# Cross-attention and experts of a decoder layer in one program, with a transition written out by hand

## What is computed

```python
x = _layernorm(x + _L0_attn_ref(x, wq, wk, wv, wo))
x = _layernorm(x + _L0_xattn_ref(x, ctx_1024, Wq, Wk, Wv, Wo, gq, gk))
    # q, k, v projected, q and k rms-normed per head, softmax(q k^T / sqrt(128)) v, times Wo
x = _layernorm(x + _L0_ffn_ref(x, gate_w, gate_bias, shared_gw, shared_dw, up_w, down_w))
    # shared: silu(g) * y @ shared_dw.T; experts: top 2 of 8 by sigmoid(x @ gate_w.T) + bias,
    # out += (silu(g_e) * u_e) @ down_w[e].T * weight
```

## Time and profile before

| | us |
|---|---|
| median of 3 runs | 1146.6 |
| lowest and highest | 1146.28, 1147.12 |
| the profiled execution | 1150.0 |
| its span, first to last instruction | 1148.3 |
| TensorE busy | 1067.5 (93%) |
| VectorE, ACT, POOL busy | 699.7, 527.4, 499.6 |
| mean granted TensorE clock | 0.961 |

### The profile page before, as it was taken

The page is one execution under the profiler, slowest core; times in us unless marked ns, Lnnn a source line. Parts: engine busy times, 40 slices in busy tenths (PEclk is TensorE's granted clock), DMA queues, the critical chain, the costliest instruction groups (busy, mean ns, idle before and its releaser), DMA issues. The chain is left out here.

```text
span 1148.3 us, 20145 instructions
## 1 busy us (share of the span) xinstructions
PE 1067.5 (93%) x7134; PEld 943.8 (82%) x7134; DVE 699.7 (61%) x1222; ACT 527.4 (46%) x1034; POOL 499.6 (44%) x462
## 2 busy tenths in 40 slices
PE   6988876999999999999999999999876979999997
PEld 5855545889999999999999999999864867777786
DVE  4267873667766766766666666667754344544447
ACT  5354542555554554454455445545432225555520
POOL 0255661755533633533533534443322334444443
PEclk9987977999999999999999999999987989999999
DMA  8001003232322323223223223222244648999943
GB/s 302 27 29 55 2 1 82 103 138 97 131 101 83 108 85 99 104 86 99 90 82 106 100 83 104 93 77 81 81 104 149 230 176 334 380 384 379 342 125 113
DMA packets 44600, 153.45 MB, mean 134 GB/s; under 512 B 3608, under 2 KB 3608, under 8 KB 41472
## 3 DMA queue, kind: packets, MB, share of 16 engines
q1 hardware_dynamic: 42304, 145.38, 35.6%
q0 software_dynamic: 2240, 7.34, 1.9%
HBM read 130.04 MB, written 22.66 MB: 133 GB/s over the span
## 5 line engine op out<-in xcount | busy, mean ns | idle before, releaser
L973 DVE TENSOR_TENSOR xa_kT_lo<-xa_turn_ps,xa_kT_hi 128x750 fp32r<-128x750 f32 x64 | 60.2, 940 | 118.4 <-ACT xa_kT_hi L896 118.4
L852 POOL TENSOR_TENSOR xa_probs<-xa_probs,xa_inv_sum 112x750 f32<-112x750 f32 x64 | 98.7, 1541 | 69.3 <-DVE xa_inv_sum L1022 69.3
L837 POOL TENSOR_TENSOR xa_k_ms<-xa_k_ss,xa_sum_eps 125x6 f32<-125x6 f32 x64 | 12.7, 198 | 257.3 <-DVE xa_k_ss L988 257.3
L86 PE MATMUL xa_k_ps<-land_xa_wk_hi,land_xa_ctx_hi 128*125 128x256 f32 x384 | 112.5, 293 | 2.8 <-PEq L177 1.7
L88 PE MATMUL xa_k_ps<-land_xa_wk_lo,land_xa_ctx_hi 128*125 128x256 f32 x384 | 109.8, 286 | 0.0
L87 PE MATMUL xa_k_ps<-land_xa_wk_hi,land_xa_ctx_lo 128*125 128x256 f32 x384 | 109.7, 286 | 0.0
L1105 PE MATMUL xa_c_ps<-xa_probsT_hi,xa_nat 125*128 125x224 f32 x384 | 93.5, 277 | 6.4 <-DMA xa_nat<-ctx_split 3.7
L1106 PE MATMUL xa_c_ps<-xa_probsT_hi,xa_nat 125*128 125x224 f32 x384 | 93.2, 277 | 0.0
L840 POOL TENSOR_TENSOR xa_k_inv<-xa_k_ms,neg_half 125x6 f32<-125x6 f32 x64 | 84.8, 1325 | 9.1 <-POOL xa_k_ms L837 7.4
L918 ACT ACTIVATE xa_probs<-xa_scores_ps,xa_bias,xa_q_scale 112x375 f32<-112x375 f32 x128 | 83.9, 661 | 9.1 <-DVE xa_bias L998 6.2
L912 ACT CAST xa_probsT_hi<-xa_turn_ps 125x672 fp32r<-125x672 f32 x64 | 46.1, 721 | 84.4 <-PE xa_turn_ps L1183 84.3
(11 more groups left out here) (287 smaller groups left out, 3275.2 us busy)
## 6 DMA issues: line engine op xcount, KB each, us to landing
xa_nat<-ctx_split SPq DMA_DIRECT2D x56, 750.0 KB
ex_raw<-in_w_units SPq DMA_DIRECT2D x15, 1408.0 KB, 8.2
ex_raw<-in_w_units SPq DMA_DIRECT2D x15, 768.0 KB, 8.0
land_ex_raw<-in_w_units SPq DMA_DIRECT2D x8, 1408.0 KB, 8.3
land_ex_raw<-in_w_units SPq DMA_DIRECT2D x8, 768.0 KB, 8.0
ctx_split<-xa_nat SPq DMA_DIRECT2D x8, 750.0 KB
sorted_x<-ex_y_sb SPq DMA_DIRECT2D x1, 5376.0 KB, 15.9
ex_x_nat<-sorted_x SPq DMA_DIRECT2D x21, 256.0 KB, 8.6
```

Of the source, the lines that this page charges most:

```text
L86: pe.matmul(out, st_hi, mv_hi, start=first, stop=False)
L852: pool.tensor_tensor(probs[0:T, u % 2], probs[0:T, u % 2], inv_sum[0:T, u % 2, :].unsqueeze(2).broadcast_to([T, 2, KV]), ALU.mult).then_in ...
L973: dve.tensor_tensor(kT_lo[:, :, 0:KV], turn_ps[:, :, 0:KV], kT_hi[:, :, 0:KV].bitcast(F32), ALU.subtract).then_inc(sem["kT_lo_done"], 1)
```

## The change

- `cross_attention` and `experts` become one function and one block, `cross_and_experts`. There is no meeting of the engines between them. `expert_views` lays the experts' buffers over those of cross-attention that are free by then.
- The context is laid out batch by batch, `ctx[:, b, 0:CC]` high and `ctx[:, b, CC:2*CC]` low, so that its space becomes free batch by batch. Self-attention's `wv_hi` and `wv_lo` get views of their own in the second half.
- SP loads the first shared unit as soon as batches 0 and 1, and then 2, have been projected for the last time (ahead of `load_nat` of units 58 and 59). ACT makes its high parts in slots 60 and 61; VectorE and POOL make its low parts, one chunk each, in slots 62 and 63 (`first_low`). `down_hi` and `down_lo` are made behind the second `dense_up`.
- The clearing of `sorted_x` is split in seven parts of 768 KB. The first stands in SP's program behind the last `store_nat` and ahead of the waits for the stores and the loads for units 8 and 9; it waits for `consts_set`, which POOL's memset of `y_sb` in slot 10 raises. The other six stand in SP's loop, one per pass, behind the sixth natural load. The gate's weights are loaded ahead of the first part and split by POOL in slot 11; POOL sets the router's constants in slot 61.
- `run_slots` ends with slot 63 (`lag` 0). What is left, up to the loop over blocks, is written out by hand for each engine. Seven banks take part in the turns; tiles 1 to 4 are normalised on POOL whole (`normalise`), output tile 6 goes to `c_ps`; TensorE interleaves the turns with the last outputs, joins and contexts, and `dense_up(0)` follows tile 4.
- The scatters go tile by tile, both choices of a tile together, each tile with a semaphore of its own, and `add_shared(t)` waits for its tile's two only. VectorE places behind `gated(1)`.

From here to the end the code is as it was, with other names.

```diff
-    v = views("land_xa", [("ctx_hi", [CC, B * KV], F32R), ("ctx_lo", [CC, B * KV], F32R), ("wk_raw", [CC, PW], F32),
+    v = views("land_xa", [("ctx", [B, 2 * CC, KV], F32R), ("wk_raw", [CC, PW], F32),
...
-        turn, turn_high, turn_low = turn_stages(nc, env, norm, norm["ln_done"], [k01_ps, k2_ps])
+        turn, turn_high, turn_low = turn_stages(nc, env, norm, norm["ln_done"], [k01_ps, k2_ps, scores_ps[:, 0], scores_ps[:, 1], k01_ps,
+                                                                                 et_ps[:, 0], et_ps[:, 1]])
...
+            def clear(g):
+                sp.dma_start(sorted_x.rearrange("(g j p) n -> g p j n", g=CLEARS, p=P)[g],
+                             y_sb[:, 0, :].unsqueeze(1).broadcast_to([P, NB // CLEARS, D])).then_inc(xs["cleared"], 16)
...
+            sp.dma_start(gate_w, gateT).then_inc(xs["gate_loaded"], 16)
+            sp.dma_start(gate_b, gate_bias.partition_broadcast(P)).then_inc(xs["gate_loaded"], 16)
+            sp.wait_ge(xs["consts_set"], 1)
+            clear(0)
             sp.wait_ge(sem["nat_0_stored"], 16 * HALF)
             sp.wait_ge(sem["nat_1_stored"], 16 * HALF)
             load_nat(0, 0, B)
...
                 for u in range(4, B + 2):
                     load_nat(u % B, i, u)
-            for u in range(N - B + 2, N):
+                    if u == 6:
+                        clear(i)
+            sp.wait_ge(sem["k_ready"], 2 * (N - B + 2))
+            sp.dma_start(raw[0][:, UP], w_units[UNIT_A, :, UP]).then_inc(xs["up_0_loaded"], 16)
+            load_nat(2, 0, N - B + 2)
+            sp.wait_ge(sem["k_ready"], 2 * (N - B + 3))
+            sp.dma_start(raw[0][:, DOWN], w_units[UNIT_A, :, DOWN]).then_inc(xs["down_0_loaded"], 16)
+            for u in range(N - B + 3, N):
                 load_nat(u % B, 0, u)
...
+                if s == B + 2:
+                    pool.memset(y_sb[:, 0, :], 0.0).then_inc(xs["consts_set"], 1)
+                if s == B + 3:
+                    split_gate()
+                if s == N - 3:
+                    set_consts()
...
+            run_slots(pool, slot, HEAD, 0, PAIRS)
...
+            normalise(1)
+            u = N - 1
+            pool.wait_ge(sem["inv_done"], N)
+            pool.tensor_tensor(probs[0:T, u % 2], probs[0:T, u % 2],
+                               inv_sum[0:T, u % 2, :].unsqueeze(2).broadcast_to([T, 2, KV]), ALU.mult).then_inc(sem["probs_done"], 1)
+            for t in (2, 3, 4):
+                normalise(t)
+            ln_power(pool, 5)
+            ln_power(pool, 6)
...
+            for t in range(TILES):
+                for k in range(2):
+                    at = k * TILES + t
+                    pool.indirect_dma_start(sorted_x, bass.IndirectOffsetOnAxis(ap=slots[:, at:at + 1], axis=0),
+                                            resid[:, t, :], None).then_inc(xs[f"scattered_{t}"], 16)
...
+            turn_probs(u - 1)
+            added(2)
+            join(N, 0, N // 2 - 2)
+            context_of(u - 1, 0)
+            turn(pe, 0)
+            pe.wait_ge(sem["probsT_lo_done"], N - 1)
+            turn_probs(u)
+            pe.wait_ge(sem["oT_lo_done"], N // 2 - 1)
+            output(3, y_ps)
+            context_of(u, 0)
+            turn(pe, 1)
+            added(3)
+            output(4, y_ps)
+            added(4)
+            join(N + 2, 0, N // 2 - 1)
+            turn(pe, 2)
+            turn(pe, 3)
+            pe.wait_ge(sem["oT_lo_done"], N // 2)
+            output(5, y_ps)
+            output(6, c_ps)
+            pe.wait_ge(norm["turn_lo"], 1)
+            turn(pe, 4)
+            pe.wait_ge(norm["turn_lo"], HALF)
+            pe.wait_ge(xs["up_lo_v"], 2)
+            pe.wait_ge(xs["up_lo_g"], 2)
             dense_up(0, 0, up_hi, up_lo)
+            turn(pe, 5)
+            turn(pe, 6)
             pe.wait_ge(norm["turn_lo"], TILES)
             logits_T()
```

More of the change, by code:

```diff
@@ L654, in ps @@
             return es.enter_context(nc.psum_tensor("xa_" + name, shape, F32))
+        v = expert_views(nc)
+        h_hi, h_lo, silu_g, h_full, y_sb = v["h_hi"], v["h_lo"], v["silu_g"], v["h_full"], v["y_sb"]
+        gate_w, gate_b, gate_hi, gate_lo = v["gate_w"], v["gate_b"], v["gate_hi"], v["gate_lo"]
+        before, every, iota_e, level, upto, iota_j = (v[n] for n in "before every iota_e level upto iota_j".split())
+        raw = [env["raw_0"], v["raw"][:, 0], v["raw"][:, 1]]
+        low = [env["low_0"], v["low"][:, 0], v["low"][:, 1]]
+        up_hi, up_lo, down_hi, down_lo, got = (env[n] for n in "up_hi up_lo down_hi down_lo got".split())
+        high = [up_hi, up_lo]
+        x_nat, xb_hi, xb_lo, h_blk, hT, logitsT = v["x_nat"], v["xb_hi"], v["xb_lo"], v["h_blk"], v["hT"], v["logitsT"]
+        score, chosen, onehot, weighed = v["score"], v["chosen"], v["onehot"], v["weighed"]
+        picked, slot_of, top_v, top_i, top_f = v["picked"], v["slot_of"], v["top_v"], v["top_i"], v["top_f"]
+        top_w, total, mix, over, run = v["top_w"], v["total"], v["mix"], v["over"], v["run"]
+        n_tiles, ends, starts, passed = v["n_tiles"], v["ends"], v["starts"], v["passed"]
+        owner_f, owner, slots_f, slots = v["owner_f"], v["owner"], v["slots_f"], v["slots"]
+        gu_ps, et_ps, ey_ps = v["gu_ps"], v["et_ps"], v["ey_ps"]
+        qT_hi, qT_lo = sb("qT_hi", [P, 2, TOK], F32R), sb("qT_lo", [P, 2, TOK], F32R)
+        q_sq = sb("q_sq", [P, 2, HT])
+        kT_hi, kT_lo = sb("kT_hi", [P, 2, KVP], F32R), sb("kT_lo", [P, 2, KVP], F32R)
+        k_sq, k_hat = sb("k_sq", [P, KT_N * PW]), sb("k_hat", [P, KT_N * PW])
+        nat_raw = sb("nat_raw", [P, 2, KT_N * CD])
         wv_raw, wo_raw = sb("wv_raw", [P, CC, PW]), sb("wo_raw", [P, 2, D])
@@ L1057, in slot, with up_low @@
                     mean_squares(0, 0)
[L1059 removed]
+            run_slots(dve, slot, HEAD, 0, PAIRS)
+            def up_low(u):
+                for c in (0, 1):
+                    cols = slice(c * CHUNK, (c + 1) * CHUNK)
+                    dve.wait_ge(xs["up_hi_done"], DC * u + c + 1)
+                    dve.tensor_tensor(low[u % RING][:, cols], raw[u % RING][:, cols], high[u % 2][:, c, :].bitcast(F32),
+                                      ALU.subtract).then_inc(xs["up_lo_v"], 1)
@@ new lines, in add_shared, with take @@
+            def add_shared(t, base):
+                n = base + t
+                dve.wait_ge(xs["y_ready"], n + 1)
+                if base == 0:
+                    dve.wait_ge(xs[f"scattered_{t}"], 32)
+                if base > 0:
+                    dve.wait_ge(xs["combined"], 2 * t + 2)
+                dve.tensor_tensor(resid[:, t, :], resid[:, t, :], ey_ps[:, n % 2, :], ALU.add).then_inc(xs["y_taken"], 1)
+            def take(j):
+                n = TILES + j
+                dve.wait_ge(xs["y_ready"], n + 1)
+                if j == 0:
+                    dve.wait_ge(xs["cleared"], 16 * CLEARS)
+                if j >= 2:
+                    dve.wait_ge(xs[f"y_{j % 2}_stored"], 16 * (j // 2))
+                dve.tensor_copy(y_sb[:, j % 2, :], ey_ps[:, n % 2, :]).then_inc(xs["y_taken"], 1)
@@ new lines, in _ @@
+            turn_low(dve, 2)
+            turn_low(dve, 3)
+            add(5, y_ps)
+            stat(5)
+            add(6, c_ps)
+            stat(6)
+            turn_low(dve, 4)
+            dve.wait_ge(norm["ln_done"], 5)
+            ln_apply(dve, 5)
+            ln_apply(dve, 6)
+            turn_low(dve, 5)
+            turn_low(dve, 6)
+            choose()
+            gated(0, 0)
+            hidden_low(0, 0)
+            gated(1, 0)
+            place()
+            hidden_low(0, 1)
@@ new lines, in _ @@
+            down_low(0, 0)
+            for k in range(2, UPS):
+                gated(k, 0)
+                hidden_low(0, k)
+            weigh()
+            for t in range(TILES):
+                add_shared(t, 0)
+            up_low(1)
+            block_low(0)
+            for j in range(NB):
+                n = UPS + j
+                up_low(j + 2)
+                dve.wait_ge(xs["silu_done"], n + 1)
+                dve.tensor_tensor(h_blk[:, 0:HID], silu_g[:, n % 2, 0:HID], gu_ps[:, n % 2, 1, 0:HID],
+                                  ALU.mult).then_inc(xs["mul_done"], 1)
+                if j + 1 < NB:
+                    block_low(j + 1)
+                if j >= 1:
+                    take(j - 1)
@@ new lines, in _ @@
+            down_low(1, LAST_U)
+            take(NB - 1)
+            gated(0, UPS + NB)
+            for k in range(1, UPS):
+                gated(k, UPS + NB)
+                hidden_low(1, k - 1)
+                for n in range(3 * k - 3, min(3 * k, GATHERS)):
+                    combine(n)
+            hidden_low(1, UPS - 1)
+            for t in range(TILES):
+                add_shared(t, TILES + NB)
+                dve.wait_ge(xs["y_taken"], TILES + NB + t + 1)
+                out_stat(dve, t)
+                if t >= 1:
+                    out_apply(dve, t - 1)
@@ L1199, in slot @@
```

(3 more changed lines are left out.)

980 lines of the change are left out of this document (483 added, 497 removed).

## The result

| | us |
|---|---|
| before, median of 19 runs | 1146.6 |
| after, median of 19 runs | 1145.1 |
| ratio, 95% interval | 0.9965 (0.9949 to 0.9981) |
| profiled execution of after, its span | 1140.1, 1138.3 |
| TensorE busy | 1056.0 (93%) |

What follows compares the result with a forecast made beforehand. TensorE hardly waits within cross-attention, but the transition from slot 64 to `block_up(0)` holds 37.3 us of idle time and low clock. Forecast: 1146.6 - 27.5 (transition) + 17.0 (stall in slot 10) = 1136.1 us, range 1129 to 1146.

Steps and rivals of the forecast that it cites:

- What bounds the kernel: TensorE hardly waits within cross-attention; the transition from slot 64 to `block_up(0)` holds 37.3 us that reordering could at most win.
- The walk of the end: Slot 64 to `block_up(0)`: 72.5 us work, 9.1 waits and 0.7 allowance give 82.3 instead of 109.8, 27.5 us less.
- VectorE 0.8 in 62 and 1.4 in 63 ... priced at nothing: Slots 62 and 63: VectorE's added work fits where engines wait for TensorE; no cost, at most 1.4 us.
- The estimate for a normalised tile on POOL: Hand-written end: normalising a tile on POOL takes about 1.1 us, bounds 0.55 and 2.0.
- The baseline of the transition: Slot 64 to `block_up(0)` before the change: 109.8 us, of which 24.0 idle and 13.3 lost to the low clock.
- 5 behind `dense_up(1)`: 5 of the 27.5 us won because the first `add_shared` no longer waits for all 14 scatters.
- The stall: Slot 10: batch 8's natural load lands 13.7 us late, the low clock loses 3.3; together 17.0 us more, bounds 14.5 to 18.
- so alone 7.2: Natural load, issue to use: 13.6 us less 6.4 for the 2176 KB behind it; 9.5 to 10 with the clearing ahead.
- the gate split that was "nothing": Slot 11: POOL's split of the gate's weights takes 0.5 us and costs nothing.
- (a): Rival: no stall in slot 10, since batches 8 and 9 load in time; 1119 us, chance 0.08.
- (b): Rival: the hand order waits more than walked and the scatter part does nothing; 5 to 9 us, 1141 to 1145, chance 0.20.
- (c): Rival: clock falls at batch 63 and stays 1.2 GHz up to `dense_up(1)`; 20 us more, 1156, chance 0.07.

Runs made afterwards that it cites:

- experiment 1: The changed kernel with the first clearing and SP's wait for it moved behind the natural loads of units 8 and 9: 1123.6 us, ratio 0.9797.
- experiments 5: The kernel of experiment 1 with POOL splitting the gate's weights in slot 61, not slot 11: 1129.9 us, ratio 0.9846.
- experiment 10: The changed kernel with SP's wait still ahead of the two natural loads, but the first clearing behind them: 1147.2 us, ratio 0.9988.
- experiments 2: The kernel before with only SP's wait for POOL's multiplication of slot 10 added ahead of unit 8's natural load: 1165.9 us, ratio 1.0157.
- number 12: The kernel before, unchanged, run again for a second profile of its transition: 1144.9 us in one run.
- 3: The changed kernel with POOL's memset of the zeroed rows one slot earlier, in slot 9: 1133.5 us, ratio 0.9879.
- 4: The changed kernel again, unaltered, as the control in the first session: 1144.8 us, ratio 0.9968.
- 8: The kernel of experiment 1 again, unaltered, as the control on the second session's chip: 1131.8 us, ratio 0.9854.
- 9: The kernel of experiment 1 with VectorE's first shared add waiting for all 14 scatters, as before the change: 1134.9 us, ratio 0.9846.
- 15: The changed kernel again, unaltered, on the third chip: 1156.1 us, ratio 1.0036.
- experiments 7: The kernel of experiment 1 with the gate split in slot 61 and tile 0 normalised early in slot 63: 1124.3 us, ratio 0.9796.
- 11: The kernel of experiments 7 again, unaltered, as a control on the third chip: 1128.4 us, ratio 0.9812.
- 14: The kernel of experiments 7 again, with both expert weight loads beside the scatters, as a control: 1131.6 us, ratio 0.9833.

## Why the prediction was wrong

The forecast was a difference of two large terms, 27.5 us less and 17.0 more. Measured in the first session they are 22.8 and 21.2. So the gain was put 4.7 us too high and the stall 4.2 too low; both errors go the same way, and what was left of 10.5 us is 1.6.

**What bounds the kernel: right.** The transition could be shortened by moving work, the slots could not, and the loop has its length otherwise: of the 25.0 us that slots 10 to 64 grew, 21.2 are the difference to experiment 1 (571.7 against 550.5).

**The walk of the end: right, but for the clock.** 82.3 us were walked, 82.7 measured in the profile of after. That was luck in part: the changed kernel takes 86.0 in the three other profiles without the hold. There TensorE idles 8.8 us (walked 9.1) and its work is 73.8 (priced at 72.5); 6.8 us at the low clock lose 3.4, and the walk had none. In experiment 1 the clock falls at 839 us, behind the wait of 2.1 us, and again at 880 us.

**"VectorE 0.8 in 62 and 1.4 in 63 ... priced at nothing": the step that failed in the transition.** The bound given for a failed cover, 1.4 us, was too low as well. Two operations that cost 0.87 and 0.52 us by themselves took 1.83 in slot 62 and 3.32 in slot 63 beside POOL's; added durations from rows where the other engine was idle can't show that. TensorE's wait was 2.1 us. In the profile of after it is 0.5; there a low-clock stretch of 3.4 us, from 852.6 us on, lies across the start of slot 64 and makes TensorE late itself, and the two others with 0.5 (experiments 5 and 10) have such a stretch at the same place. The estimate for a normalised tile on POOL, 1.1 us within 0.55 and 2.0, was also too low: each takes 2.1. No wait of TensorE follows from it.

**The baseline of the transition: mis-sized.** The 109.8 us came from one execution. Two more of the same code in the transition (experiments 2 and 12, number 12 on another chip and with ACT held) take 105.6 and 106.0, with 8.5 and 12.5 us less at the low clock. So up to 4 of the 27.5 us were the clock's luck in that one profile. It can't be said more closely: that profile is of a run 3.4 us above the median of its kernel, the other two are of runs 8.8 and 4.1 below theirs. By the profiles the term is 19.6 to 23.7 us (105.6 and 109.7 less 86.0).

**"5 behind `dense_up(1)`": right on one chip, nothing on another.** Without the hold the wait fell by 3.1 us (3.7 to 0.6) and a low-clock stretch with it. With it, the late silu takes the place of the scatters. It was not the finer semaphores alone either: in experiment 1 all scatters had landed at 904.43, 0.4 us after the first add began. Both kernels need 22.3 to 23.8 us from the first of the next units' loads to there; but VectorE is ready for the first add 22.1 us behind that load (904.0 - 881.9) and no longer 20.5 (924.2 - 903.7), since its weighing and the last silus come later in the new order.

**The stall: right in place and mechanism, too small by 4.** POOL's memset, SP's wait, the wait in slot 10 and the low clock behind it came as told. The terms: the memset ends 3.3 us behind the time at which the context is due (forecast 3.5); issuing the clearing 0.5 (0.5); issue to use 12.3 instead of 9.5 to 10. The failed step is "so alone 7.2". That the loads behind it had lengthened batch 63's 13.6 us was right in kind, by the table under experiment 10. But the 6.4 us of the 2176 KB were taken off whole, as if they had stood ahead, and they had added only 4: without them the load takes 9.6 us (experiment 10), and the trace of before had its last packet 8.7 us behind the issue in slot 10. The clearing ahead adds 1.3 and not 2.0. The other 1.4 up to 12.3 were not in the sum: by the packets they go to the next weights' loads, which now run beside this one. So the wait is 3.3 + 0.5 + 12.3 = 16.1 us. The clock: 3.3 forecast, 3.0 lost behind the wait. Then

- slot 12's second fall, 6.8 us long in the profile of after, loses 3.4 (in experiment 1 its 3.4 us lose 1.7), and goes with the gate split that was "nothing";
- 16.1 + 3.0 + (3.4 - 1.7) = 20.8 us, against 21.2 measured.

**The rivals.** (a), no stall, didn't come, but experiment 1 is the kernel that it describes: 1123.6 us, forecast 1119. (b) was nearest in number and in part in mechanism: low clock in the end, and an add that wins nothing on some chips. 1145.1 is its upper end. It had 0.20, and had not been combined with a stall larger than forecast. (c), a tail at 1.2 GHz, fell: the transition has 2.4 us of low clock in the profile of after, 14.4 at most in those of the change in 1, 3, 4, 8, 9 and 15.

**The version that beats both** is that of experiments 7, 11 and 14: 2.0, 1.9 and 1.7% faster than before in three sessions, 1124.3 us where before takes 1148.6. Experiment 1, without the two moves, is 2.0% faster on the first chip and 1.5% on the second.

## What to carry to other kernels

A load that a pipeline needs in a fixed slot must not stand behind a wait for another engine's work of that same slot; move the wait behind the load, and look for this first when a preparation is pulled into a running loop. Price an operation on VectorE or POOL that is put into "idle" time by what the other of the two does there, not by its own duration alone. Before a stretch with falls of the clock is taken as the baseline, have a second profile of it: here up to 4 of 27 us were one execution's. A transfer's own length is read where nothing runs beside it, not by taking off what ran beside it.

## What the runs showed of the hardware

- VectorE and POOL hold each other up: the same normalisation of 128x512 takes 0.52 us with POOL idle and 3.32 beside its multiplication and low part (2.01 and 1.69 us).
- A stall costs more than its wait. After 16 us the clock was 0.5 for another 6.0 us of work; by the stage that holds it a stall of 5.4 us costs 7.3 in all, one of 16 us 21.
- The same kernel differs by chip in a way that its neighbour doesn't: experiment 1 takes 1123.6 and 1131.8 us on two chips, before 1146.4 and 1148.6. On two of three chips ACT starts one or two activations up to some 6 us late while indirect DMAs scatter rows; the cause is open.
- A DMA of zeroed rows (768 KB) issued ahead of a load by the same queue delays its first packet by 1.3 us, issued behind it not at all. Loads of 2176 KB issued behind lengthen the packets of the load ahead from 139 to 217 ns and its time from issue to use from 9.6 to 13.6 us.
